# First layer of a two-layer conv kernel: the 42 channels' share of the last product in plain fp32 column tiles, the first depthwise tap added to the inverse transform, and the nine taps kept within a tile

## The reference, cut to what matters

```python
def _L0_conv_ref(x, w_in, w_dw, fft_weight, w_out):     # DIM 64, HID 170, P 8
    h = einsum('oi,bihw->bohw', w_in, x)
    gate, x_sp, x_fr = split(h, 3, axis=1)              # 170 channels each
    sp = depthwise_conv_3x3(x_sp, w_dw)
    f = rfft2(blocks of 8 x 8 pixels of x_fr) * fft_weight
    fr = irfft2(f)                                      # back to pixels
    fused = gelu(gate) * (sp + fr)
    return einsum('oi,bihw->bohw', w_out, fused)        # 170 -> 64 channels
x = x + _L0_conv_ref(group_norm(x), ...)
x = x + _L1_conv_ref(group_norm(x), ...)                # layer 1, not touched
```

## Time and profile before

| | PE | PEld | DVE | ACT | POOL |
|---|---|---|---|---|---|
| busy, us | 9574.8 | 7178.7 | 8528.6 | 6300.8 | 1810.0 |
| share of the span | 92% | 69% | 82% | 61% | 17% |
| instructions | 73254 | 73254 | 12871 | 10071 | 1824 |

### The profile page before, as it was taken

How to read it: one execution, slowest core, us unless ns; L and a number is a source line. 1 busy time by engine, 2 the same in 40 slices (tenths; PEclk the granted TensorE clock), 3 DMA queues, 4 the chain that set the end, 5 groups by cost and what they waited for, 6 DMA issues and landing times.

```text
span 10369.4 us, 189285 instructions
## 1 busy us (share of the span) xinstructions
PE 9574.8 (92%) x73254; PEld 7178.7 (69%) x73254; DVE 8528.6 (82%) x12871; ACT 6300.8 (61%) x10071; POOL 1810.0 (17%) x1824
## 2 busy tenths in 40 slices
PE   1999988999899998898989999899898999989998
PEld 1677765857777775675877777577686777658667
DVE  7788878978788887887878888788886888789787
ACT  0666654656766665554776666555586666546557
POOL 0000003333300001333320000223341000033334
PEclk9999999999999999998999999899999999999999
DMA  4667665475677766447567776635566666663655
GB/s 114 146 142 147 142 145 188 175 225 147 157 151 143 147 142 175 166 168 226 155 152 147 143 146 138 207 146 192 182 175 129 131 130 130 123 213 157 218 158 155
DMA packets 1332968, 1652.32 MB, mean 159 GB/s; under 512 B 844252, under 2 KB 1077100, under 8 KB 1246700
## 3 DMA queue, kind: packets, MB, share of 16 engines
q1 hardware_dynamic: 1332076, 1640.22, 61.5%
HBM read 786.84 MB, written 515.00 MB: 126 GB/s over the span
## 4 chain that ended last, share of the span: by engine, by line
PE 68%; DVE 18%; ACT 5%; issue 5%; DMA 1%; SPq 1%; POOL 1%; DVEq 0%; ACTq 0%; POOLq 0%
PE ps L821 14%; PE ps L1752 7%; PE ps L788 6%; PE ps L1765 5%; PE ps L779 4%; PE ps L835 4%; DVE S L1534 3%; PE ps L1330 3%; PE ps L854 3%; PE ps L1402 3%; PE ps L879 2%; PE ps L866 2%; DVE S L1877 2%; DVE tq L1697 2%; PE ps L815 2%
## 5 line engine op out<-in xcount | busy, mean ns | idle before, releaser
L1150 DVE SCALAR_TENSOR_TENSOR F<-U,LW,F 106x512 f32<-106x512 f32 x2048 | 1535.9, 750 | 54.5
L1752 PE MATMUL ps<-fp,Dwr 128*128 128x512 f32 x6144 | 1474.6, 389 | 0.0
L1752 PEld LDWEIGHTS ps<-fp,Dwr 128*128 128x128 f32 x6144 | 1153.1, 188 | 240.2
L1128 DVE TENSOR_TENSOR Z<-ps,LW 128x340 f32<-128x340 f32 x1024 | 523.1, 511 | 743.4 <-PE ps L788 723.1
L821 PE MATMUL ps<-P,WP 128*128 128x512 f32 x3072 | 905.8, 417 | 31.5 <-DMA H<-P 31.5
L1765 PE MATMUL ps<-XP,Cwr 128*128 128x512 f32 x3072 | 835.6, 408 | 95.0 <-DVE XP L1889 95.0
L1330 PEld LDWEIGHTS ps<-RS,Bc 128*128 128x128 f32 x4096 | 585.0, 200 | 484.6 <-DVE RS L1319 298.0
L821 PE MATMUL ps<-H,WP 128*128 128x512 f32 x3072 | 916.9, 420 | 0.0
L1402 PE MATMUL ps<-fp,Bwr 128*128 128x512 f32 x3072 | 878.7, 426 | 21.3 <-DVE fp L1503 21.3
L948 ACT ACTIVATE XF<-ps 128x340 f32<-128x340 f32 x1024 | 466.6, 456 | 683.0 <-PE ps L779 682.1
L1840 ACT ACTIVATE x<-ps,cst 128x512 f32<-128x512 f32 x512 | 352.2, 688 | 833.2 <-PE ps L1765 796.6
(11 more groups left out here) (296 smaller groups left out, 20440.0 us busy)
## 6 DMA issues: line engine op xcount, KB each, us to landing
H<-P SPq DMA_DIRECT2D x512, 585.0 KB, 7.2
raw<-x SPq DMA_DIRECT2D x240, 640.0 KB, 11.5
fx_d<-fx SPq DMA_DIRECT2D x112, 1024.0 KB, 4.0
fl_d<-fp SPq DMA_DIRECT2D x112, 1024.0 KB, 5.6
fp<-fl_d SPq DMA_DIRECT2D x112, 1024.0 KB, 5.7
fx<-fx_d SPq DMA_DIRECT2D x112, 1024.0 KB, 5.4
x1h_d<-xo SPq DMA_DIRECT2D x256, 256.0 KB, 9.0
x1v_d<-xo SPq DMA_DIRECT2D x512, 128.0 KB, 8.0
```

Of the source, the lines that this page charges most:

```text
L1128: e.tensor_tensor(Z[t % 2][:, 2 * c:2 * c + 2, :].rearrange("p a b -> p (a b)"), ps[6][:, 0:2 * HID], Wt, ALU.mult).then_inc(sem["z"], 1)
L1150: ins = e.scalar_tensor_tensor(o, u, wd[0:106, i:i + 1], o, ALU.mult, ALU.add)
L1752: ins = e.matmul(bank(m)[:], Dwr[:, w, c:c + 128], fq[n % 2][x][:, s2, :], start=(s2 == 0 and w == 0 and x == 0), stop=False)
```

## The change

Three things, all in layer 0:

1. In `wout` the three fp32r products of the 42 channels over the full width give way to two plain fp32 ones of 64 columns, each in its half of the array, straight from `F42` and the unsplit weights `wo42`. With that `fh42`, `fl42`, the tiles `FP42` and `WO`, and what fills them, go.
2. Tap 0 becomes a multiply and add whose addend is ps[4], the inverse transform. `fu42`'s addition goes. So tap 0 of tile t now waits for `finv42(t)`, and `finv42(t)` waits for tap 0 of tile t-1 to have read the bank.
3. `finv42(t)` moves ahead, right behind `gate(t, 0)` and `gate(t, 1)`. The taps of tile t all run within iteration t: 0 and 1 at its start, 2 and 3, 4 and 5 between the `z` steps, 6 to 8 and `fu42(t)` at its end.

```diff
@@ wout, finv42 (PE)
         def finv42(t):
             e.wait_ge(sem["z"], 4 * (NT * b + t) + 4)
             if t:
-                e.wait_ge(sem["ad"], NT * b + t)
+                e.wait_ge(sem["tap"], 9 * (NT * b + t - 1) + 1)
...
-            e.wait_ge(sem["fl42"], NT * b + t + 1)
-            for w, x in PARTS:
-                ins = e.matmul(ps[7][:], WO[w][:], FP42[s][x][:], start=False, stop=(w == 1), skip_group_check=True)
+            e.wait_ge(sem["fu42"], NT * b + t + 1)
+            for p in range(2):
+                ins = e.matmul(ps[7][64 * p:64 * p + 64, :], wo42[:, 64 * p:64 * p + 64], F42[s][:], start=False, stop=True,
+                               skip_group_check=True)
             ins.then_inc(sem["wout"], 1)
@@ the loop of l0_pe
             if t:
                 gate(t, 0)
                 gate(t, 1)
+            finv42(t)
+            if t:
                 conv(t, 0, range(2, 5))
...
-            if t == NT - 1:
-                finv42(t)
             wout(t - 1)
             fs(t + 1, 2)
             pointwise(t + 1, 2)
             conv(t + 1, 0, range(1))
             xs(t + 1, 3)
-            if t < NT - 1:
-                finv42(t)
             conv(t + 1, 0, range(1, 2))
             fs(t + 1, 3)
@@ the loop of l0_act
             xf(t + 1, 0)
-            fh42(t - 1)
...
-        fh42(NT - 1)
@@ wp1 (ACT), wp2 (DVE)
-        e.activation(WO[0][:], wo42, ACT.Copy)
...
-        e.tensor_tensor(WO[1][:], wo42, WO[0][:].bitcast(F32), ALU.subtract)
@@ depthwise, fu42, fl42 (DVE)
                 if i == 0:
                     e.wait_ge(sem["uc"], 3 * (NT * b + t) + 3)
-                    ins = e.tensor_scalar(o, u, wd[0:106, 0:1], None, ALU.mult)
+                    e.wait_ge(sem["fi42"], NT * b + t + 1)
+                    if t >= 2:
+                        e.wait_ge(sem["wout"], NT * b + t - 1)
+                    v = ps[4][0:106, :].rearrange("c (a w) -> c a w", a=4)
+                    ins = e.scalar_tensor_tensor(o, u, wd[0:106, 0:1], v, ALU.mult, ALU.add)
...
         def fu42(t):
-            e.wait_ge(sem["fi42"], NT * b + t + 1)
             e.wait_ge(sem["tap"], 9 * (NT * b + t + 1))
-            e.tensor_tensor(F42[t % 2][:], ps[4][0:106, :], F42[t % 2][:], ALU.add).then_inc(sem["ad"], 1)
-            e.wait_ge(sem["ad"], NT * b + t + 1)
             e.wait_ge(sem["ge42"], NT * b + t + 1)
             e.tensor_tensor(F42[t % 2][:], F42[t % 2][:], G42[t % 2][:], ALU.mult).then_inc(sem["fu42"], 1)
@@ the loop of l0_dve
-        depthwise(0, range(4))
         for t in range(NT):
+            depthwise(t, range(2))
             z(t + 1, 0)
-            depthwise(t, range(4, 7))
+            depthwise(t, range(2, 4))
             fu(t, 0)
             fu(t, 1)
             z(t + 1, 1)
-            fl42(t - 1)
-            depthwise(t, range(7, 9))
+            depthwise(t, range(4, 6))
             z(t + 1, 2)
             if t == NT - 1:
+                depthwise(t, range(6, 9))
                 fu42(t)
             x1(t - 1)
...
             p2(t + 2)
             z(t + 1, 3)
-            if t < NT - 1:
-                fu42(t)
-            else:
-                fl42(t)
...
             bn(t - 1)
-            depthwise(t + 1, range(4))
+            if t < NT - 1:
+                depthwise(t, range(6, 9))
+                fu42(t)
```

More of the change, by code:

```diff
@@ L224, in build @@
     F42 = [at(f"F42{i}", [106, 512]) for i in range(2)]
-    FP42 = [[at(f"FQ{i}{p}", [106, 512], F32R) for p in range(2)] for i in range(2)]
-    WO = [at(f"WO{i}", [106, 128], F32R) for i in range(2)]
     xo = [at(f"xo{i}", [128, 2048]) for i in range(2)]
@@ L960, in ge42 @@
             e.activation(G42[t % 2][:], ps[5][0:106, :], ACT.Gelu).then_inc(sem["ge42"], 1)
[L962 to L968, removed]
         def uc(t, k):
```

## The result

The changed kernel takes 10423.49 us (median of 5, 10422.03 to 10426.13); the kernel before, in 5 runs beside it, 10382.38 us. The ratio is 1.0041, 95% interval 1.0026 to 1.0056: 41 us slower by the medians, 27 to 58 by the interval. The forecast was 10429, +46, slower. The profiled execution of the changed kernel has a span of 10424.3 us, 54.9 more than that of before, whose profiled execution (10371.16 us) was faster than all five beside it.

The account below looks back on a forecast made before the run. Layer 0 was taken to cost what PE's list costs, 256 tiles one after another. 256 x 0.17 = 43.5 plus 2.5 for the ends gave +46 us on 10382.97, 10429 us; range 10398 to 10478.

Parts of the forecast that it names:

- Part 1, the product: Last product in `wout`: four fp32 column-half products up to `fs` take 1.98 us instead of 1.81, +0.17 us a tile.
- inner phase of 0.43 us: `wout`: each phase between the first and last of the column-half pairs costs 0.43 us, read from the last tile's L879.
- rival (b): `wout`: the second pair's weight loads aren't hidden, adding 0.27 us a tile; +115 us, 10498; chance 0.05.
- the bound below: `wout`: both halves' phases shrink to an fp32r product's 0.23 us, making the part worth -0.23 us a tile.
- Rival (c): `wout`: the two column halves don't run side by side, two more phases of 0.43 us; +264 us, 10649; chance 0.03.
- Part 2, DVE and ACT: Split and addition removed: frees DVE some 1.1 us and ACT 0.6 us a tile, costed at nothing.
- Part 3, `finv42`: Moved `finv42`: 0.11 us lost at one `fs`, regained at the other; net 0, between -0.05 and +0.1 us.
- wait for `z` behind the gate: Moved `finv42(t)` needs `z(t, 3)`; PE's wait for it was forecast as met with 0.1 us to spare.
- Rival (a): Moved `finv42` does wait and the exposed load isn't regained: 0.06 to 0.19 us a tile more, 10444 to 10478; chance 0.17.
- Rival (e): Layer 0 paced by the ring through DVE, `p2`, `xb`, `xr`, first `xf`: -0.2 us a tile, 10333; chance 0.05.
- (d): Exposed loads at first and second `fs` close: net -0.05 to +0.08 us a tile, 10370 to 10403; chance 0.10.
- Ends: End of each image: DVE's way to the last `x1` grows by 0.6 us, 2.5 us in all.

Follow-up runs that it names:

- the edit alone: Kernel before with only `wout` changed to two plain fp32 column halves, without the split; taps, addition and `finv42` as before: 10419.9 us, ratio 1.0032.
- the run that closed the last `fs`: Changed kernel with one of the first convolution block's three products moved behind the tile's last `xs`: 10435.4 us, ratio 1.0047 to the kernel before.
- four such moves: Kernel before with `finv42` next to `wout`, one conv product behind last `xs`, `p2` ahead of `x1`, `rows` between ACT's `p1` and third `uc`: 10286.14 us, ratio 0.9909.

## Why the prediction was right, and where it was off

**What bounds it.** Right for the product and for the work that the change moves: the product costs what PE's rows said, and the split's work on DVE and ACT moves nothing, taken off or given back. Too strong as it stands: "layer 0 costs what PE's list costs" leaves out that from the third `fs` of a tile to the next tile's first one the ring through DVE and ACT was 0.08 us longer than PE's list. The prediction saw its trace, the open load at the first `fs`, and took it for an idle place of PE rather than for the end of a ring. None of the work that the change takes off lies on this ring; that is why it is worth nothing, and not that DVE and ACT have air.

**Part 1, the product.** +0.17 forecast, +0.162 measured in the stretch and +0.166 for the edit alone. The step that carried it was the inner phase of 0.43 us, taken from the last tile's L879 behind `finv42`. L880 begins 0.90 us after L877, which is 0.48 + 0.43: the loads of the second pair are hidden. With that rival (b) falls. The rule behind it, in the Trainium skill ("TensorE: Matmul & The Clock Gate", Part 3), that a load overlaps only when its row group differs, doesn't hold here: the loads of the next pair, same rows of the array, run while the pair before still streams (609.32, against 609.74 for its products). The same Part also names a background weight buffer as a target for which loads are pulled ahead, which the prediction left out; no run here shows which buffer a load takes. One figure of that part was misread without harm: 0.155 us a record of `fs`, in the bound below. The group behind `fs` is recorded as starting almost with its second record (608.09 + 0.73 - 0.45 = 608.37, against 608.40), so a record of 340 columns takes 0.28 us; the difference between an open and a closed `fs`, on which the sum rests, isn't touched by that. Rival (c) falls with the same rows: the four records of L880 span 1.03 us, the two halves side by side.

**Part 2, DVE and ACT.** Costed at nothing, measured at nothing (0.004 us a tile with the work put back). Tap 0 with its addend in PSUM takes 0.741 us, in the bounds.

**Part 3, `finv42`.** Here the sum was off, by 0.04 us a tile, 10 us in all. I had put the last `fs`'s new open load (0.06 to 0.11) against the first `fs`'s closed one (0.11) and called it 0. The former is 0.11, of which 0.064 is in `fs` itself and 0.05 ahead of it. The latter gave back 0.074: I had read it off one tile (0.42 less 0.31), and the median over the tiles is 0.386 less 0.313. The term was mis-sized because it came from one row where a median was to be had. Of its -0.05 to +0.1 it came out at +0.04; the other terms were right, so this isn't a forecast saved by two errors against each other.

The wait for `z` behind the gate was forecast as met "with 0.1 us to spare". It is met with nothing to spare: `z` started later than I had put it, and about 0.01 us a tile is lost there. Rival (a) was right about the place and wrong about the price. That it binds was then shown by the run that closed the last `fs` and gained nothing.

**Rival (e)**, the ring through `p2`, `xb` and the first copy, was closer to the truth than its chance of 0.05 says, though not in its sign. In the kernel before the ring sets the part of the tile from the third `fs` to the first one, 0.08 us above PE's list; in the changed kernel it has dropped behind. With `finv42` moved out of it the tile grows by 0.88 us. Its relief brought nothing because no step of it was relieved. The argument against it ("`z` idles 0.88 us right behind `p2`") was about a side branch: the branch that counts goes on to `xb`. And (d)'s gain at the first `fs` was real (31 us in the kernel before), but it is had by order and not by less work.

**Ends.** The last two `wout` starts of an image lie 6.02 us apart before (1473.94 and 1479.96) and 6.49 after (1486.65 and 1493.14): +0.47 against +0.6 forecast.

**Sum.** +46 forecast; +52 by the tiles, +41 by the medians. The profiled execution was to be 10417 us and took 10426. That the median lies under the forecast while the tiles lie over it is scatter between executions and no merit of the forecast.

## What to carry to other kernels

Where one engine's list sets the stage, price a rewrite in that engine's start-to-start times, and look for the same instruction elsewhere in the trace in the surroundings that it will get (the last tile had it); what the rewrite takes off other engines is worth only the idle places that the bound engine has for them. Those places are made by order: moving one step of another engine behind the copy that TensorE waits for brought 31 us here, four such moves 97, while 377 us less work on two engines, none of it on the ring that mattered, brought none. A chain that is PE to 99% doesn't rule such a ring out; a load that waits a little in every tile points to it, and start-to-start times between two fixed steps, compared over runs, show it. Before a step is moved out of a gap, add up the ring that the gap was filling, each of its branches, and what is queued behind each new wait, on the DMA queue too.

## What the runs showed of the hardware that was not expected

- DVE's next step doesn't always begin at the same distance from the recorded end of the one before, though nothing idles between. `z` began 0.03 us after `p2`'s end (614.87 and 614.90), and in the run with `p2` ahead of `x1` 0.03 us after `x1`'s (632.11 and 632.14), where L1156 in the kernel before begins 0.08 us before the end of `z` (613.46 against 613.54). The length of the step before doesn't decide it: in the kernel before, L1150 begins 0.04 us after the 0.46 us of L1147, whose result it waits for. In both cases of `z` the last DVE step that read PSUM before it was the second half of `x1`, which reads from partition 64 on, where `z` reads from partition 0. The two halves of `x1` themselves, at partitions 0 and 64, take 1.38 us together, and the two steps of `fu`, both at partition 0 and just as long (0.68 us each), 1.28. That fits a price for changing the partition that the reading starts at, but no run varies it. A margin of 0.1 us can't be taken from such rows without a row for the same pair of steps.
- `finv42` followed by `wout`, both in column halves, costs less than each between full-width products: 0.93 us for `finv42` in place of 1.03, and 0.96 for L879 in place of 1.01.
- SyncE's queue held a 585 KB transfer back behind a wait for another buffer, for 11.8 us in the tile shown, and every other tile grew from 18.1 to about 29.8 us.
